# A decoder layer with sparse experts: a third buffer for raw expert weights, and a small load of its own for each slot's place and weight

## The chip, the cores and the metric

One core of a Trainium2 chip runs the whole kernel in one launch. The metric is the device time of one execution, in microseconds (us).

## The reference

The input is 32 sequences of 128 tokens with 256 channels (4096 tokens). Three blocks follow one another, each with a residual sum and a layer norm behind it: self-attention with 16 heads, cross-attention with one head onto a second input, and a feed-forward block that has an attention of its own and then a mixture of experts. The part that matters here is the last one:

```python
probs = jax.nn.softmax(h2 @ router_w, axis=-1)            # 8 experts
topw, topi = jax.lax.top_k(probs, 2)
topw = jax.nn.softmax(topw, axis=-1)
combine = jnp.sum(jax.nn.one_hot(topi, 8) * topw[..., None], axis=1)
shared = (silu(h2 @ sh_gate) * (h2 @ sh_up)) @ sh_down    # 256 -> 512 -> 256
gate = jnp.einsum('td,edf->etf', h2, e_gate)
up = jnp.einsum('td,edf->etf', h2, e_up)
eout = jnp.einsum('etf,efd->etd', jax.nn.silu(gate) * up, e_down)
out = layernorm(x2 + X + shared + jnp.einsum('etd,te->td', eout, combine))
```

Each token goes through the shared network and through the two experts that the router picks for it. All is float32.

## The kernel before, in words

**Two phases.** Phase A does the three attentions for 16 pairs of sequences by a schedule that is written out by hand. It is not touched. Phase B does the experts. It works in 55 *units* of 256 tokens, all with the same matrix products: first 13 units of the shared network (`BEFORE = 13`, a unit is a pair of sequences), then 39 *tiles* of routed tokens (`TILES`), then the last 3 shared units. A tile holds up to 256 tokens that go to one expert; which expert that is, is read at run time from `expert_table`, so its weights are loaded anew for each tile, 3 x 512 KB (gate, up, down).

**Products in split precision.** A float32 product is made of three products of rounded operands. ScalarE writes the rounded weights `we_hi` (`split`, L1257), VectorE the rest `we_lo` (`split_lo`, L1417), both from the raw weights `w_raw`, in the order down weights of tile n (kind 2), then gate and up weights of tile n+1 (kinds 0 and 1), all within unit n. TensorE then does, per unit n: gate and up for half the hidden channels (`gate_up(n, 0)`, 24 matmuls, L1204), the transposes of the tokens of unit n+1 (`turn(n+1)`, 4 matmuls, L1184), `gate_up(n, 1)`, and the down product of unit n-1 (`down_unit`, 24 matmuls, L1220). The activation between them passes ScalarE (silu and rounding, L1273 and L1280), VectorE (product, L1433) and GpSimd (the rest, `routed_lo`, L1561), and `down_unit(n)` waits for the last of it.

**Routing.** During the shared units VectorE works out each token's two slots. GpSimd scatters token rows into the scratch tensor `slots` by indirect DMAs (`scatter`, L1537). A row has 258 floats: 256 channels, its place in the output and its weight. `load_slots(i)` on SyncE loads the 256 rows of tile i into one of two buffers `slot_rows`. `read_meta(i)` on GpSimd then copies weight (L1556) and place (L1557, with a cast to an integer) into small rings of four, `slot_weight` and `slot_place`, so that the row buffer can be loaded again. When tile i has its down product, VectorE multiplies it by the weight into one of three `y_rows` (L1456), and GpSimd adds the rows to the scratch tensor `total` at their places by two indirect DMAs that accumulate (`add_tile`, L1572); it first waits until those of the tile before have landed (`y_added`).

**The raw weights.** `w_raw` has two buffers. `load_expert(i)` (L1137) fills buffer (i + 1) % 2. Tiles 0 and 1 are loaded early. After that SyncE goes through a loop, in order: wait for the transposes of tile i and for `meta_done` of tile i (L1153), `load_slots(i + 2)` (L1141), wait for the split of the down weights of tile i, the last reader of its buffer (L1135), `load_expert(i + 2)`. SyncE works in order, and all its loads go through one hardware queue (q1). The indirect DMAs of GpSimd go through another (q0).

**GpSimd's order** in unit n (tile i) is: `routed_lo(n, 0)`, `add_tile(i - 2)`, `read_meta(i + 1)`, `routed_lo(n, 1)`. At the end come the last two `add_tile`, then loads of `total` into `acc` that accumulate (L1593), and the last layer norm.

Of the kernel before, what the change touches and what calls it, by code (L numbers as in the profile page):

```python
# [17 lines left out]
F32 = mybir.dt.float32  # L18
# [29 lines left out]
ROW = D + 2  # L48
METAS = 4
KINDS = ("w_gate", "w_up", "w_down")  # L50
# [927 lines left out]
def phase_b(nc, t, scratch, sem, kept, all_stored, out):  # L978
# [6 lines left out]
    with ctx:  # L985
# [23 lines left out]
        y_rows = kept["late"][:, :].rearrange("p (i j d) -> p i j d", i=3, j=2)  # L1009
        place = sb("place", [P, B])  # L1010
        slot_weight = sb("slot_weight", [P, METAS, 2])
        slot_place = sb("slot_place", [P, METAS, 2], I32)

# [41 lines left out]
        h_loaded = [kept["loaded"], *(sem(f"h_loaded{g}") for g in range(1, GROUPS))]  # L1055
        raw_loaded = [sem(f"w_loaded{i}") for i in range(2)]
        rows_loaded = [sem(f"rows_loaded{i}") for i in range(2)]
# [16 lines left out]
        total_loaded = [sem(f"total_loaded{g}") for g in range(len(TOTALS))]  # L1074
        meta_done = sem("meta_done")
        var_done, eps_b_done, rstd_b_done, norm_done, out_stored = (
# [8 lines left out]
        def raw_of(use):  # L1085
            return kept["weights"] if use == 0 else w_raw[:, use % 2]

# [16 lines left out]

        totals = scratch["total"][0:P * B, :].rearrange("(p b) d -> p b d", p=P)

        def low_products(k):
# [6 lines left out]
        with nc.Block() as block:  # L1114

            @block.sync
            def _(sp):
                sp.dma_start(consts, t["route"]).then_inc(loaded, 16)
                sp.dma_start(tri[:, :], t["tri"]).then_inc(loaded, 16)
                sp.dma_start(place[:, :], t["place"]).then_inc(loaded, 16)  # L1120

                def load_rows(g):
                    b = slice(g * GB, (g + 1) * GB)
                    sp.dma_start(rows_of(b)[:, :, 0:D], scratch["h2"][:, b, :]).then_inc(h_loaded[g], 16)

                for g in range(1, GROUPS):
                    if g == GROUPS - 1:
                        all_stored(sp)
                    load_rows(g)

                def tile_rows(name, i):
                    return scratch[name][i * UT:(i + 1) * UT, :].rearrange("(j p) d -> p j d", p=P)

                def load_expert(i):
                    e = sp.value_load(expert_table[0:1, i:i + 1], min_val=1, max_val=E)  # L1135
                    for k, n in enumerate(KINDS):
                        sp.dma_start(w_raw[:, (i + 1) % 2, k, :], t[n][bass.ds(e, 1), :, :].rearrange("a p n -> (a p) n"))\  # L1137
                          .then_inc(raw_loaded[(i + 1) % 2], 16)

                def load_slots(i):  # L1140
                    sp.dma_start(slot_rows[:, i % 2, :, :], tile_rows("slots", i)).then_inc(rows_loaded[i % 2], 16)  # L1141

                sp.wait_ge(table_done, 1)
                load_expert(0)
                sp.wait_ge(w_lo_done, 3)
                load_expert(1)
                for i, batches in enumerate((B // 2, B // 2, B)):
                    sp.wait_ge(scattered[i], 16 * batches)
                for i in range(2):
                    load_slots(i)  # L1150
                for i in range(TILES - 2):
                    sp.wait_ge(turned_done, FIRST_TILE + i + 1)
                    sp.wait_ge(meta_done, 2 * i + 2)  # L1153
                    load_slots(i + 2)
                    sp.wait_ge(w_lo_done, split_count(FIRST_TILE + i, 2))
                    load_expert(i + 2)


                sp.wait_ge(y_added, 16 * 2 * TILES)
                sp.wait_ge(w_lo_done, split_count(AFTER_TILES - 1, 2))  # L1160

                b = slice(2 * BEFORE, B)
                sp.dma_start(acc[:, b, :], totals[:, b, :]).then_inc(total_loaded[total_of[BEFORE]], 16)
                for pair in range(PAIRS):
                    sp.wait_ge(norm_done, pair + 1)
                    sp.dma_start(out[:, 2 * pair:2 * pair + 2, :], acc[:, 2 * pair:2 * pair + 2, :]).then_inc(out_stored, 16)
                sp.wait_ge(out_stored, 16 * PAIRS)

            @block.tensor
            def _(pe):  # L1170
                def turn(n):
                    i = tile_of(n)
                    if i is None:
                        g = pair_of(n) * 2 // GB
                        pe.wait_ge(h_loaded[g], 16 if g else KEPT)
                        src = rows_of(slice(2 * pair_of(n), 2 * pair_of(n) + 2))
                    else:
                        pe.wait_ge(rows_loaded[i % 2], 16 * (i // 2 + 1))
                        src = slot_rows[:, i % 2, :, :]
# [66 lines left out]
            def _(act):  # L1246
                def split(n, kind):
                    i = tile_of(n)
                    w_hi, _ = weights_of(n)
                    use = 0 if i is None else i + 1  # L1250
                    act.wait_ge(*((kept["loaded"], KEPT) if use == 0 else (raw_loaded[use % 2], 48 * ((use + 1) // 2))))
# [5 lines left out]
                    act.activation(w_hi[:, kind, :], raw_of(use)[:, kind, :], ACT.Copy).then_inc(w_hi_done, 1)  # L1257

# [66 lines left out]
            def _(dve):  # L1325
# [86 lines left out]
                def split_lo(n, kind):  # L1412
# [3 lines left out]
                    dve.wait_ge(w_hi_done, split_count(n, kind))  # L1416
                    dve.tensor_tensor(w_lo[:, kind, :], raw_of(use)[:, kind, :], w_hi[:, kind, :].bitcast(F32),  # L1417
                                      ALU.subtract).then_inc(w_lo_done, 1)
# [21 lines left out]
                def read_down(n):  # L1440
# [10 lines left out]
                    else:  # L1451
                        if i >= 3:
                            dve.wait_ge(y_added, 16 * 2 * (i - 2))
                        dve.wait_ge(meta_done, 2 * i + 1)
                        for j in range(2):
                            ins = dve.tensor_scalar(y_rows[:, i % 3, j, :], src[:, j, :], slot_weight[:, i % METAS, j:j + 1], None, ALU.mult)  # L1456
                        ins.then_inc(down_read, 1)
# [60 lines left out]
            def _(pool):  # L1518
                pool.memset(ones[:, :], 1.0).then_inc(ones_b_set, 1)
                pool.memset(half_power[:, :], -0.5).then_inc(pool_set, 1)  # L1520
                pool.wait_ge(loaded, 16 * 3)
                pool.tensor_copy(kept["rows"][:, :, D], place[:, 0:GB]).then_inc(pool_set, 1)
                pool.tensor_copy(h_rows[:, :, D], place[:, GB:B]).then_inc(pool_set, 1)
                pool.wait_ge(pool_set, 3)
# [40 lines left out]
                def add_tile(i):  # L1565

                    pool.wait_ge(down_read, FIRST_TILE + i + 1)
                    pool.wait_ge(meta_done, 2 * i + 2)
                    if i > 0:
                        pool.wait_ge(y_added, 16 * 2 * i)  # L1570
                    for j in range(2):
                        pool.indirect_dma_start(  # L1572
                            out=scratch["total"], out_offset=bass.IndirectOffsetOnAxis(ap=slot_place[:, i % METAS, j:j + 1], axis=0),
                            in_=y_rows[:, i % 3, j, :], in_offset=None, compute_op=ALU.add).then_inc(y_added, 16)

                read_meta(0)
                for n in range(FIRST_TILE, AFTER_TILES):
                    i = tile_of(n)
                    routed_lo(n, 0)
                    if i >= 2:  # L1580
                        add_tile(i - 2)
                    if i + 1 < TILES:
                        read_meta(i + 1)
                    routed_lo(n, 1)
                add_tile(TILES - 2)
                add_tile(TILES - 1)

                pool.wait_ge(y_added, 16 * 2 * TILES)
                for g, pairs in enumerate(TOTALS):
# [51 lines left out]
def layout(inputs):  # L1641
# [29 lines left out]
    def route_constants():  # L1671
# [19 lines left out]
        "route": route_constants(),  # L1691
        "empty": (np.eye(1, ROW, D) * (B * S + np.arange(ROWS))[:, None]).astype(np.float32),
        "place": (B * np.arange(P)[:, None] + np.arange(B)).astype(np.float32),
        "wqk1": rows(np.concatenate([by_channel(a("L0_attn_Wq")), by_channel(a("L0_attn_Wk"))]).T),
# [30 lines left out]
```

## Time and profile before

| | us |
|---|---|
| median of 3 runs | 1162.86 (1160.27 to 1165.91) |
| the profiled execution's own time | 1166.36 |
| its span in the trace | 1164.6 |
| TensorE busy | 1080.5 (93% of the span) |
| VectorE, ScalarE, GpSimd busy | 800.5, 623.7, 572.5 |
| mean granted clock of TensorE | 0.971 of full speed |

How to read it: the busy time of TensorE is modelled and overlaps, so that 93% does not mean that nothing can be won. The span begins with phase A; phase B begins at about 615 us, and its 39 tiles take the time from about 740 to 1108 us. Of the DMAs of phase B the page gives the median time from issue to landing: 3.5, 4.5 and 6.6 us for the gate, up and down weights of one tile (512 KB each, all three issued within 1 us), 5.0 us for the slot rows (258 KB), 6.5 us for an accumulating indirect DMA.

### The profile page before, as it was taken

Reading aid. Unit: us, or ns where it says so; the run is one execution under the profiler, and the core shown is the slowest. Engines: PE = TensorE matmul, PEld = TensorE weight load, DVE = VectorE, ACT = ScalarE, POOL = GpSimd, SP = SyncE. Lnnn points to the kernel's source line nnn. Section 1 sums busy time; section 2 is a strip of 40 time slices with the busy share of each in tenths; the row PEclk is TensorE's granted clock in tenths of the full one; section 3 lists DMA queues with packets and bytes.
Section 4 is the critical chain, followed back from the end, with each engine's and each line's share of the span. In section 5 each row is a group of like instructions: output and inputs, shape, how many; then the busy total and the mean of one; then the engine's idle time right before and its main releaser. Section 6 shows DMA issues by size and latency. Waiting matters only on the chain. (4 is left out here: it accounts for less than half of the span.)

```text
span 1164.6 us, 32771 instructions
## 1 busy us (share of the span) xinstructions
PE 1080.5 (93%) x13012; PEld 1014.7 (87%) x13012; DVE 800.5 (69%) x1367; ACT 623.7 (54%) x1266; POOL 572.5 (49%) x620
## 2 busy tenths in 40 slices
PE   3889999999999999999777999999999999999992
PEld 3678888999888998999666999999999999999992
DVE  1668778777878777787646644567777777677646
ACT  1244555555555655566534333566666666666635
POOL 4243333344433334443210677356666676666664
PEclk8899999999999999999976999999999999999996
DMA  7585454444555444440304422267777777777648
GB/s 204 103 191 109 90 110 93 118 115 81 129 111 102 113 107 94 76 75 29 110 27 158 182 101 97 92 216 219 222 227 218 218 218 230 237 213 221 183 77 244
DMA packets 284071, 167.64 MB, mean 144 GB/s; under 512 B 210081, under 2 KB 255393, under 8 KB 283041
## 3 DMA queue, kind: packets, MB, share of 16 engines
q1 hardware_dynamic: 267456, 140.97, 44.1%
q0 software_dynamic: 14880, 22.09, 9.5%
q10 hardware_dynamic: 1584, 2.49, 0.6%
q8 instruction: 104, 1.70, 0.6%
q14 instruction: 47, 0.38, 0.1%
HBM read 121.66 MB, written 54.15 MB: 151 GB/s over the span
## 5 line engine op out<-in xcount | busy, mean ns | idle before, releaser
L1572 POOL DMA_INDIRECT total_scratch<-kept_late,slot_place x78 | 143.5, 1840 | 90.7 <-DMA total_scratch<-kept_late,slot_place 70.8
L1433 DVE TENSOR_TENSOR prod<-kept_weights,up 128x512 f32<-128x512 f32 x110 | 75.2, 684 | 145.0 <-ACT kept_weights L1273 145.0
L1561 POOL TENSOR_TENSOR act_lo<-prod,act_hi 128x512 fp32r<-128x512 f32 x78 | 120.5, 1596 | 40.5 <-ACT act_hi L1280 40.5
L1257 ACT ACTIVATE we_hi<-w_raw 128x1024 fp32r<-128x1024 f32 x117 | 117.9, 1048 | 26.6 <-DMA w_raw<-in_w_down 26.6
L1273 ACT ACTIVATE kept_weights<-gate 128x512 f32<-128x512 f32 x110 | 65.0, 591 | 110.7 <-PE up L1204 110.7
L1280 ACT ACTIVATE act_hi<-prod 128x512 fp32r<-128x512 f32 x110 | 69.5, 632 | 91.2 <-DVE prod L1433 89.9
L677 ACT ACTIVATE p3t<-psum 128x512 f32<-128x512 f32 x128 | 68.8, 595 | 88.6 <-PE psum L526 88.6
L928 POOL TENSOR_TENSOR ctx_lo<-ctx_t,ctx_hi 128x512 fp32r<-128x512 f32 x16 | 20.6, 1285 | 140.1 <-ACT ctx_hi L587 140.1
L1417 DVE TENSOR_TENSOR we_lo<-w_raw,we_hi 128x1024 fp32r<-128x1024 f32 x60 | 78.8, 1341 | 13.2 <-ACT we_hi L1257 11.6
L848 DVE TENSOR_REDUCE max<-psum 128x16 f32<-128x2048 f32 x32 | 73.3, 2292 | 18.2 <-PE psum L512 18.2
L367 PE MATMUL psum<-kept_room,x_hi 128*128 128x512 f32 (+1 forms) x256 | 63.4, 372 | 17.9 <-POOL x_lo L924 17.9
L1417 DVE TENSOR_TENSOR we_lo_place<-w_raw,we_hi 128x1024 fp32r<-128x1024 f32 x57 | 74.4, 1331 | 5.0 <-ACT we_hi L1257 3.5
L1204 PE MATMUL gate<-tok_hi,we_hi 128*128 128x256 f32 x312 | 67.5, 298 | 11.0 <-DVE we_lo L1417 7.9
L367 PEld LDWEIGHTS psum<-kept_room,x_hi 128*128 128x128 f32 x256 | 43.4, 202 | 25.7 <-issue 21.2
L1537 POOL DMA_INDIRECT slots_scratch<-h_rows,slot_index x56 | 55.0, 982 | 16.7 <-issue 12.5
L871 DVE RECIPROCAL rden<-psum 128x256 f32<-128x256 f32 x32 | 56.2, 1757 | 10.1 <-PE psum L539 10.1
L1204 PE MATMUL up<-tok_lo,we_hi 128*128 128x256 f32 x312 | 62.7, 283 | 0.0
L1204 PE MATMUL up<-tok_hi,we_hi 128*128 128x256 f32 x312 | 62.5, 282 | 0.0
L1204 PE MATMUL gate<-tok_lo,we_hi 128*128 128x256 f32 x312 | 62.5, 282 | 0.0
L1204 PEld LDWEIGHTS gate<-tok_hi,we_hi 128*128 128x128 f32 x312 | 47.6, 189 | 15.0 <-issue 14.7
L924 POOL TENSOR_TENSOR x_lo<-x_t,x_hi 128x512 fp32r<-128x512 f32 x16 | 20.4, 1275 | 67.0 <-ACT x_hi L583 66.9
L935 POOL TENSOR_TENSOR x_res<-x_res,b_o 128x512 f32<-128x512 f32 x16 | 21.0, 1311 | 61.0 <-DMA x_res<-in_x 61.0
(273 smaller groups left out, 3403.7 us busy)
## 6 DMA issues: line engine op xcount, KB each, us to landing
w_raw<-in_w_gate SPq DMA_DIRECT2D x39, 512.0 KB, 3.5
w_raw<-in_w_up SPq DMA_DIRECT2D x39, 512.0 KB, 4.5
w_raw<-in_w_down SPq DMA_DIRECT2D x39, 512.0 KB, 6.6
slots_scratch<-in_empty SPq DMA_DIRECT2D x39, 258.0 KB, 3.4
kept_weights<-slots_scratch SPq DMA_DIRECT2D x39, 258.0 KB, 5.0
x_t<-in_x_t SPq DMA_DIRECT2D x16, 256.0 KB, 3.3
q_scratch<-qk SPq DMA_DIRECT2D x16, 256.0 KB, 2.4
k_scratch<-qk SPq DMA_DIRECT2D x16, 256.0 KB, 2.9
```

What stands on the lines that cost most here:

```text
L367: mm = pe.matmul(dst, x(dk), y(dk), start=(n == 1), stop=(n == 3 * DK))
L677: act.activation(p3t[:, a, 4 * j:4 * j + 4, :], bank[f"s3t_{a}"][:, 512 * j:512 * (j + 1)].rearrange("p (h n) -> p h n", h=4), ACT.Exp)\
L848: half_step(dve.tensor_reduce(max3[:, a, :], bank[f"s3_{a}"].rearrange("p (h n) -> p h n", h=H), AX.X, ALU.max, negate=True))
L871: half_step(dve.reciprocal(rden3[:, a, :], bank[f"pv3_{a}"][:, DK * S:2 * DK * S]))
L1204: mm = pe.matmul(bank[:, fi * UT:(fi + 1) * UT], wp[:, kind, dk * DFF + f * P:dk * DFF + (f + 1) * P], hp[:, n % 2, dk, :], start=(m == 1) ...
L1257: act.activation(w_hi[:, kind, :], raw_of(use)[:, kind, :], ACT.Copy).then_inc(w_hi_done, 1)
L1273: act.activation(silu[:, h, :], gate[h][:, :], ACT.Silu).then_inc(silu_done, 1)
L1280: act.activation(act_hi[:, n % 2, h * FH:(h + 1) * FH, :], prod[:, h, :].rearrange("p (f n) -> p f n", f=FH), ACT.Copy).then_inc(act_hi_do ...
L1417: dve.tensor_tensor(w_lo[:, kind, :], raw_of(use)[:, kind, :], w_hi[:, kind, :].bitcast(F32), ALU.subtract).then_inc(w_lo_done, 1)
L1433: dve.tensor_tensor(prod[:, h, :], silu[:, h, :], up[h][:, :], ALU.mult).then_inc(prod_done, 1)
L1561: pool.tensor_tensor(act_lo[:, n % 2, h * FH:(h + 1) * FH, :], prod[:, h, :].rearrange("p (f n) -> p f n", f=FH), act_hi[:, n % 2, h * FH: ...
L1572: pool.indirect_dma_start(out=scratch["total"], out_offset=bass.IndirectOffsetOnAxis(ap=slot_place[:, i % METAS, j:j + 1], axis=0), in_=y_ ...
```

## The change

1. Raw weights get a third buffer. Its gate weights lie in a new tensor `raw_gate`, its up and down weights in the part of `h_rows` that held the rows of sequences 16 to 23, which were scattered and transposed by then. Uses of the buffers go round by three.
2. `load_slots(i)` also loads place and weight of the 256 slots into a ring `slot_meta` of six, by a DMA of its own: two runs of 8 bytes in each of 128 partitions. `rows_loaded` now counts 32 for a tile instead of 16. `read_meta` with its two copies goes, and `meta_done` with it. VectorE, and GpSimd's `add_tile`, read `slot_meta` in its place. Place is an integer from the start.
3. SyncE's loop has another order: `load_slots(i)` waits for the transposes of tile i-2 and, from tile 6, for the added rows of tile i-6; then the split of the down weights of tile i-2 is waited for, and `load_expert(i + 1)` follows. Tile 2 is loaded ahead of the loop.

```diff
-METAS = 4
+METAS = 6
+RAW_FROM = 12
...
-        place = sb("place", [P, B])
-        slot_weight = sb("slot_weight", [P, METAS, 2])
-        slot_place = sb("slot_place", [P, METAS, 2], I32)
+        place = sb("place", [P, B], I32)
+        slot_meta = sb("slot_meta", [P, METAS, 2, ROW - D])
+        raw_gate = sb("raw_gate", [P, WC])
+        sent = h_rows[:, :, :].rearrange("p b d -> p (b d)")[:, RAW_FROM * ROW:RAW_FROM * ROW + 2 * WC]
+        raws = [[w_raw[:, 1, k, :] for k in range(3)], [w_raw[:, 0, k, :] for k in range(3)],
+                [raw_gate[:, :], sent[:, 0:WC], sent[:, WC:2 * WC]]]
...
+        def added_upto(i):
+            return 2 * i
...
-                        sp.dma_start(w_raw[:, (i + 1) % 2, k, :], t[n][bass.ds(e, 1), :, :].rearrange("a p n -> (a p) n"))\
-                          .then_inc(raw_loaded[(i + 1) % 2], 16)
+                        sp.dma_start(raws[i % 3][k], t[n][bass.ds(e, 1), :, :].rearrange("a p n -> (a p) n"))\
+                          .then_inc(raw_loaded[i % 3], 16)
                 def load_slots(i):
+                    if i >= 2:
+                        sp.wait_ge(turned_done, FIRST_TILE + i - 1)
+                    if i >= METAS:
+                        sp.wait_ge(down_read, FIRST_TILE + i - METAS + 1)
+                        sp.wait_ge(y_added, 16 * added_upto(i - METAS + 1))
                     sp.dma_start(slot_rows[:, i % 2, :, :], tile_rows("slots", i)).then_inc(rows_loaded[i % 2], 16)
+                    sp.dma_start(slot_meta[:, i % METAS, :, :], tile_rows("slots", i)[:, :, D:ROW]).then_inc(rows_loaded[i % 2], 16)
                 sp.wait_ge(table_done, 1)
                 load_expert(0)
-                sp.wait_ge(w_lo_done, 3)
                 load_expert(1)
                 for i, batches in enumerate((B // 2, B // 2, B)):
                     sp.wait_ge(scattered[i], 16 * batches)
-                for i in range(2):
+                load_slots(0)
+                load_slots(1)
+                sp.wait_ge(turned_done, (GB + RAW_FROM + 2 * WC // ROW) // 2 + 1)
+                load_expert(2)
+                for i in range(2, TILES):
                     load_slots(i)
-                for i in range(TILES - 2):
-                    sp.wait_ge(turned_done, FIRST_TILE + i + 1)
-                    sp.wait_ge(meta_done, 2 * i + 2)
-                    load_slots(i + 2)
-                    sp.wait_ge(w_lo_done, split_count(FIRST_TILE + i, 2))
-                    load_expert(i + 2)
+                    if i + 1 < TILES:
+                        sp.wait_ge(w_lo_done, split_count(FIRST_TILE + i - 2, 2))
+                        load_expert(i + 1)
...
-                        pe.wait_ge(rows_loaded[i % 2], 16 * (i // 2 + 1))
+                        pe.wait_ge(rows_loaded[i % 2], 32 * (i // 2 + 1))
...
-                        dve.wait_ge(meta_done, 2 * i + 1)
+                        dve.wait_ge(rows_loaded[i % 2], 32 * (i // 2 + 1))
...
-                def read_meta(i):
-                    pool.wait_ge(rows_loaded[i % 2], 16 * (i // 2 + 1))
-                    if i >= METAS:
-                        k = i - METAS
-                        pool.wait_ge(down_read, FIRST_TILE + k + 1)
-                        pool.wait_ge(y_added, 16 * 2 * (k + 1))
-                    pool.tensor_copy(slot_weight[:, i % METAS, :], slot_rows[:, i % 2, :, D + 1]).then_inc(meta_done, 1)
-                    pool.tensor_copy(slot_place[:, i % METAS, :], slot_rows[:, i % 2, :, D]).then_inc(meta_done, 1)
...
                 def add_tile(i):
                     pool.wait_ge(down_read, FIRST_TILE + i + 1)
-                    pool.wait_ge(meta_done, 2 * i + 2)
+                    pool.wait_ge(rows_loaded[i % 2], 32 * (i // 2 + 1))
```

## Rows read from the trace of the kernel before

**Rows 1.** The page, part 1: engine, busy us, share of the span, instructions.

```profile
PE 1080.5 (93%) x13012; PEld 1014.7 (87%) x13012; DVE 800.5 (69%) x1367; ACT 623.7 (54%) x1266; POOL 572.5 (49%) x620
```

**Rows 2.** Busy us per stretch (PE, PEld, DVE, ACT, POOL), clock, DMA share, GB/s.

```profile
737.72:1105.85 368.13, 357.11 (x2964) 353.16 (x2965) 262.54 (x349) 232.47 (x349) 243.20 (x226) 1.00 0.72 211
```

**Rows 3.** Waits from 740 to 1110: engine and line, for whom, us, times, longest.

```profile
ACT we_hi L1257 <- DMA w_raw<-in_w_down: 26.6, 27, 2.4
...
PE gate L1204 <- DVE we_lo L1417: 7.9, 10, 1.6
```

**Rows 4.** The chain that ended last: start us, us, what, two tiles of it.

```profile
884.53 7.42 DMA w_raw<-in_w_down
891.97 1.07 ACT we_hi L1257
893.07 1.24 DVE we_lo L1417
894.44 1.67 PE gate L1204 x12
...
899.48 1.05 ACT we_hi L1257
900.55 1.50 DVE we_lo L1417
903.68 7.24 DMA w_raw<-in_w_down
```

**Rows 5.** PE in order of time: one tile's transposes, of 40 such rows these five.

```profile
737.72 0.66 PE L1184 MATMUL turned<-ident,kept_weights 128*128 128x128 f32 x4 [0.78 <-DMA kept_weights<-slots_scratch]
...
859.22 0.60 PE L1184 MATMUL turned<-ident,kept_weights 128*128 128x128 f32 x4
868.21 0.60 PE L1184 MATMUL turned<-ident,kept_weights 128*128 128x128 f32 x4
...
982.01 0.60 PE L1184 MATMUL turned<-ident,kept_weights 128*128 128x128 f32 x4
...
1105.85 0.60 PE L1184 MATMUL turned<-ident,h_rows 128*128 128x128 f32 x4
```

**Rows 6.** SyncE's queue in order of time: the first slot rows, two expert loads.

```profile
734.99 0.38 SPq L1141 DMA_DIRECT2D kept_weights<-slots_scratch  x1
...
978.36 0.34 SPq L1137 DMA_DIRECT2D w_raw<-in_w_gate  x1
...
987.39 0.34 SPq L1137 DMA_DIRECT2D w_raw<-in_w_gate  x1
```

**Rows 7.** GpSimd in order of time, one tile; last, idle before it and its releaser.

```profile
978.62 1.77 POOL L1572 DMA_INDIRECT total_scratch<-kept_late,slot_place  x1 [2.08 <-DMA total_scratch<-kept_late,slot_place]
980.69 1.55 POOL L1572 DMA_INDIRECT total_scratch<-kept_late,slot_place  x1 [0.30 <-issue]
981.94 1.87 POOL L1561 TENSOR_TENSOR act_lo<-prod,act_hi 128x512 fp32r<-128x512 f32 x1
...
987.90 1.75 POOL L1572 DMA_INDIRECT total_scratch<-kept_late,slot_place  x1 [2.33 <-DMA total_scratch<-kept_late,slot_place]
```

**Rows 8.** Small runs in phase A: eight loads of 512 runs of 64 bytes.

```profile
L329 SPq DMA_DIRECT2D vbd<-v_scratch x8: 485/486/2675, 299.3 to 305.9; - x8
...
DMA to landing us min/median/max: 2.5/2.5/4.9
```

**Rows 9.** The same loads: busy us per stretch as in Rows 2, DMA share second to last.

```profile
304.00:305.00 1.00, 1.00 (x10) 1.00 (x9) 0.87 (x2) 1.00 (x3) 1.00 (x2) 1.00 0.44 46
```

**Rows 10.** VectorE and GpSimd in order of time, where both read at once.

```profile
1041.62 2.08 DVE L1417 TENSOR_TENSOR we_lo_place<-w_raw,we_hi 128x1024 fp32r<-128x1024 f32 x1
...
1039.51 3.11 POOL L1561 TENSOR_TENSOR act_lo<-prod,act_hi 128x512 fp32r<-128x512 f32 x2
```

**Rows 11.** Groups from 740 to 1110: line, engine, operation, count, busy us, mean ns.

```profile
L1556 POOL COPY slot_weight<-kept_weights 128x2 f32<-128x2 f32 x38 | 30.3, 798 | 0.0
```

**Rows 12.** GpSimd at the end of the tiles: one accumulating DMA.

```profile
1109.57 2.36 POOL L1572 DMA_INDIRECT total_scratch<-kept_late,slot_place  x1 [0.15 <-issue]
```

More of the change, by code:

```diff
@@ L1055, in phase_b @@
         h_loaded = [kept["loaded"], *(sem(f"h_loaded{g}") for g in range(1, GROUPS))]
-        raw_loaded = [sem(f"w_loaded{i}") for i in range(2)]
+        raw_loaded = [sem(f"w_loaded{i}") for i in range(3)]
         rows_loaded = [sem(f"rows_loaded{i}") for i in range(2)]
@@ L1074, in phase_b @@
         total_loaded = [sem(f"total_loaded{g}") for g in range(len(TOTALS))]
-        meta_done = sem("meta_done")
         var_done, eps_b_done, rstd_b_done, norm_done, out_stored = (
@@ L1085, in raw_of @@
         def raw_of(use):
-            return kept["weights"] if use == 0 else w_raw[:, use % 2]
+            return [kept["weights"][:, k, :] for k in range(3)] if use == 0 else raws[(use - 1) % 3]
         FIRST_TILE, AFTER_TILES = BEFORE, BEFORE + TILES
@@ L1148, in _ @@
                     sp.wait_ge(scattered[i], 16 * batches)
-                for i in range(2):
-                    load_slots(i)
-                for i in range(TILES - 2):
-                    sp.wait_ge(turned_done, FIRST_TILE + i + 1)
-                    sp.wait_ge(meta_done, 2 * i + 2)
-                    load_slots(i + 2)
-                    sp.wait_ge(w_lo_done, split_count(FIRST_TILE + i, 2))
-                    load_expert(i + 2)
-                sp.wait_ge(y_added, 16 * 2 * TILES)
+                load_slots(0)
[3 more added lines that the diff above has]
+                for i in range(2, TILES):
+                    load_slots(i)
+                    if i + 1 < TILES:
+                        sp.wait_ge(w_lo_done, split_count(FIRST_TILE + i - 2, 2))
+                        load_expert(i + 1)
+                sp.wait_ge(y_added, 16 * added_upto(TILES))
                 sp.wait_ge(w_lo_done, split_count(AFTER_TILES - 1, 2))
@@ L1250, in split @@
                     use = 0 if i is None else i + 1
-                    act.wait_ge(*((kept["loaded"], KEPT) if use == 0 else (raw_loaded[use % 2], 48 * ((use + 1) // 2))))
+                    act.wait_ge(*((kept["loaded"], KEPT) if use == 0 else (raw_loaded[(use - 1) % 3], 48 * ((use - 1) // 3 + 1))))
                     if i is not None and i >= 2:
@@ L1256, in split @@
                             act.wait_ge(down_ready, n - 1)
-                    act.activation(w_hi[:, kind, :], raw_of(use)[:, kind, :], ACT.Copy).then_inc(w_hi_done, 1)
+                    act.activation(w_hi[:, kind, :], raw_of(use)[kind], ACT.Copy).then_inc(w_hi_done, 1)
                 def token_hi(n):
@@ L1416, in split_lo @@
                     dve.wait_ge(w_hi_done, split_count(n, kind))
-                    dve.tensor_tensor(w_lo[:, kind, :], raw_of(use)[:, kind, :], w_hi[:, kind, :].bitcast(F32),
+                    dve.tensor_tensor(w_lo[:, kind, :], raw_of(use)[kind], w_hi[:, kind, :].bitcast(F32),
                                       ALU.subtract).then_inc(w_lo_done, 1)
@@ L1452, in read_down @@
                         if i >= 3:
-                            dve.wait_ge(y_added, 16 * 2 * (i - 2))
-                        dve.wait_ge(meta_done, 2 * i + 1)
+                            dve.wait_ge(y_added, 16 * added_upto(i - 2))
+                        dve.wait_ge(rows_loaded[i % 2], 32 * (i // 2 + 1))
                         for j in range(2):
-                            ins = dve.tensor_scalar(y_rows[:, i % 3, j, :], src[:, j, :], slot_weight[:, i % METAS, j:j + 1], None, ALU.mult)
+                            ins = dve.tensor_scalar(y_rows[:, i % 3, j, :], src[:, j, :], slot_meta[:, i % METAS, j, 1:2], None, ALU.mult)
                         ins.then_inc(down_read, 1)
@@ L1521, in _ @@
                 pool.wait_ge(loaded, 16 * 3)
-                pool.tensor_copy(kept["rows"][:, :, D], place[:, 0:GB]).then_inc(pool_set, 1)
-                pool.tensor_copy(h_rows[:, :, D], place[:, GB:B]).then_inc(pool_set, 1)
+                pool.tensor_copy(kept["rows"][:, :, D].bitcast(I32), place[:, 0:GB]).then_inc(pool_set, 1)
+                pool.tensor_copy(h_rows[:, :, D].bitcast(I32), place[:, GB:B]).then_inc(pool_set, 1)
                 pool.wait_ge(pool_set, 3)
@@ L1567, in add_tile @@
                     pool.wait_ge(down_read, FIRST_TILE + i + 1)
-                    pool.wait_ge(meta_done, 2 * i + 2)
+                    pool.wait_ge(rows_loaded[i % 2], 32 * (i // 2 + 1))
                     if i > 0:
-                        pool.wait_ge(y_added, 16 * 2 * i)
+                        pool.wait_ge(y_added, 16 * added_upto(i))
                     for j in range(2):
                         pool.indirect_dma_start(
-                            out=scratch["total"], out_offset=bass.IndirectOffsetOnAxis(ap=slot_place[:, i % METAS, j:j + 1], axis=0),
+                            out=scratch["total"], out_offset=bass.IndirectOffsetOnAxis(ap=slot_meta[:, i % METAS, j, 0:1].bitcast(I32), axis=0),
                             in_=y_rows[:, i % 3, j, :], in_offset=None, compute_op=ALU.add).then_inc(y_added, 16)
-                read_meta(0)
                 for n in range(FIRST_TILE, AFTER_TILES):
@@ L1581, in _ @@
                         add_tile(i - 2)
-                    if i + 1 < TILES:
-                        read_meta(i + 1)
                     routed_lo(n, 1)
@@ L1586, in _ @@
                 add_tile(TILES - 1)
-                pool.wait_ge(y_added, 16 * 2 * TILES)
+                pool.wait_ge(y_added, 16 * added_upto(TILES))
                 for g, pairs in enumerate(TOTALS):
@@ L1691, in layout @@
         "route": route_constants(),
-        "empty": (np.eye(1, ROW, D) * (B * S + np.arange(ROWS))[:, None]).astype(np.float32),
-        "place": (B * np.arange(P)[:, None] + np.arange(B)).astype(np.float32),
+        "empty": (np.eye(1, ROW, D, dtype=np.int32) * (B * S + np.arange(ROWS, dtype=np.int32))[:, None]).view(np.float32),
+        "place": (B * np.arange(P)[:, None] + np.arange(B)).astype(np.int32),
         "wqk1": rows(np.concatenate([by_channel(a("L0_attn_Wq")), by_channel(a("L0_attn_Wk"))]).T),
```

## The prediction

> **What bounds the kernel now.** I read the page first: TensorE is busy 93% of the span, the others 69% and less [rows 1]. So time can only come from TensorE's waits, or from the ends of the phases. Only the tiles are touched, so I next took the stretch from the first tile's transposes to those of the first shared unit behind the tiles, 737.72 to 1105.85 us: 368.13 us for 39 tiles, 9.44 us each, with TensorE busy 357.11 us at a granted clock of 1.00 [rows 2, 5]. Then I read the starts of the transposes one by one, since one unit follows the other there. The quickest tiles take 8.99 us, as from 859.22 to 868.21 [rows 5], and then TensorE waits for nobody. A tile that takes longer waits for the rest of the gate weights from VectorE, and that work waits, over ScalarE, for the raw weights: 26.6 us of waiting on ScalarE in 27 of the tiles [rows 3].
>
> The chain of waits shows the loop that does it [rows 4]. Down weights are issued at 884.53 and take 7.42 us to land, ScalarE and VectorE split the gate weights (1.07 and 1.24 us), the gate products begin at 894.44, then come the two splits of the down weights, and at 903.68 down weights are issued again. That is 19.15 us for two tiles, 9.57 each, against 8.99 of matrix work. With two buffers a tile's load starts only when the tile two before it has been split, so this loop goes round once in two tiles and TensorE cannot be faster than it.
>
> **The change, part by part.** *The third buffer.* Tile i+1 is now issued after the split of tile i-2, where before it was after that of tile i-1: one unit, 9 us, earlier. The same loop now spreads over three tiles: 19.15 / 3 = 6.4 us per tile, below 8.99. So the stall goes whole, and the matrix work is late next. What does a tile then take? From below 8.99 us [rows 5]. From above 9.44, if something of the same size is right behind. I take 9.05, near the quick tiles, with 0.06 for an occasional short wait. Sum: 39 x (9.44 - 9.05) = 15.2 us; the ends are 17.5 us (all tiles at 8.99) and 0.
>
> *The DMA queues.* The DMA engines are busy 0.72 of the stretch [rows 2], 0.72 x 368.13 / 39 = 6.8 us per tile. The small load adds 256 runs of 8 bytes. The nearest rows are loads of 512 runs of 64 bytes, issued (305.9 - 299.3) / 7 = 0.94 us apart [rows 8] at a share of 0.44 [rows 9]: 0.41 us for 512 runs, so some 0.2 us for 256. 7.0 of 9.05 us leaves the engines idle for 2 us per tile: nothing on the path. Below, the cost is zero; above, the share in the row would be all due to latency and each run would cost as much whatever its size, still 0.4. SyncE pays one more issue of 0.49 us a tile [rows 8], and it waits most of the time.
>
> *What is queued behind the new waits on SyncE.* Tile i's slot rows now ask for the added rows of tile i-6, and the next expert load stands behind them. Adds of a tile start about 0.3 to 0.5 us behind an expert issue and the next tile's adds, which wait for their landing, start 9.3 us later (978.62 to 987.90) [rows 6, 7]. So the adds of tile i-6, issued in unit i-4, have landed when SyncE asks in unit i-3, or do so within a microsecond. The expert load behind is due only a unit later. Zero, with 8 us of cover. The slot rows themselves go out behind 1.5 MB of weights now, but are wanted some 18 us later.
>
> *GpSimd loses two copies a tile*, 0.8 us each [rows 11], partly beside each other. It waits 2.33 us for its adds right afterwards [rows 7]: the freed time becomes waiting. The wait for `meta_done` on SyncE stands before the slot rows, not between a split and its expert load. Both at zero. What they could give at most is that the last part of the activation is ready earlier, for which TensorE does not wait. The other readers (VectorE's factor, the offsets of the adds) wait for a count that the transposes have already waited for: zero.
>
> *The first tile.* Here alone slot rows are on the path: issued at 734.99, landed just before 737.72, TensorE idle 0.78 us for them [rows 5, 6]. The transposes now wait for the small load too, issued some 0.45 us later. The 64-byte loads land in 2.5 us at least and mostly, 4.9 at most [rows 8]: 737.9 or 740.3 against 737.7, so +0.3 to +2.7 us. I take +0.5, by the median and a little for the rows ahead of it. The Trainium skill ("DMA: Bandwidth & Descriptors", rules for kernel authors) speaks against such loads: below 64 KB one pays mostly overhead. By its fit of 2.0 us per DMA the small load would land at 737.4, before the rows, and this term would be zero; that fit is for DMAs issued from GpSimd, and no run here shows it for SyncE.
>
> *The end.* The adds of the third last tile start 0.15 us behind GpSimd's own product, at 1109.57 [rows 12], so no load held them. The chain of adds and the final norm move with TensorE. Zero.
>
> Net: -15.2 + 0.5 = -14.7 us. The profiled execution took 1166.36 us (1.8 us beside its span of 1164.6), so it would take 1151.7. It is 3.5 us above the median of the runs shown, 1162.86; the same 14.7 off that median gives 1148.2 us, my prediction.
>
> **Rivals.** *A: GpSimd and VectorE take the stall's place.* An add waits for the landing of the one before, and this one seems bound to the end of the weights' traffic: 987.90 is 9.54 us behind the expert issue at 978.36 and 0.51 behind the next at 987.39 [rows 6, 7]. If each tile takes 9.05, adds start 0.5 us behind an issue, the following product of GpSimd ends 5.2 us later (978.62 to 983.81), 5.7 behind the issue. The down product wants it at 985.3 or so: 982.01, plus the transposes (0.3) and half of the gate and up products (24 of 74 equal matmuls of 8.99, 2.9 us) [rows 5], that is 6.9 behind the issue. Cover is 1.2 us. Small loads that stretch the traffic by 0.2 us leave 1.0. But if the adds slip further, two products of GpSimd run back to back (3.11 us) and the split of the down weights beside them takes 2.08 us in place of 1.50 [rows 4, 10], which puts the gate weights late. The Trainium skill ("SBUF — State Buffer", who interferes with whom) has it that a VectorE instruction with two inputs in SBUF contends with a GpSimd one that reads SBUF; the trace agrees with its 2.08 against 1.50. For: the tiles around 980 take above 9.03. Against: their waits too are for weights. At 9.2 us a tile: 39 x 0.24 = 9.4, less 0.5: 1154.0.
>
> *B: no gain.* Expert loads are not earlier, because SyncE gets stuck at the adds of tile i-6, or they are and the traffic is merely spread. For it: all loads stand in one queue behind one waiting engine. Against: 8 us of cover, above. Time: 1162.9 + 0.5 = 1163.4.
>
> *C: slower, by the small runs.* An 8-byte run could cost far more than a 64-byte one. Then the queue never runs dry, and a tile takes 6.8 us plus the small load. From 2.6 us on (165 ns a run and engine; the row gives 0.41 x 16 / 512 = 13 ns) this is above 9.44. At 3.5 us: 10.3 a tile, 39 x 0.86 = +33.5, with the start 1196.9. For: no row shows runs of 8 bytes. Against: a factor of 13.
>
> **How the numbers follow.** Forecast 0.67 (its own range 1144 to 1152), A 0.17, B 0.09, C 0.07. About 0.5% (5.8 us) is what this measurement tells from no change. Faster: the forecast and nearly all of A, 0.83; same: B and the rest of A, 0.10; slower: C, 0.07. The range from 1144 to 1157 holds the forecast (17.5 us off and a little noise: 1144) and A with its noise; B and C are left out, 0.16.
>
> **What would show it.** Right: ScalarE no longer waits for the down weights at L1257 in the tiles; transposes 8.99 to 9.1 us apart all along; an expert issue every 9.0 us, landed more than 5 us before ScalarE wants it; DMA share near 0.77; GpSimd waits for its adds about 2 us in each tile; TensorE idle 1.0 to 1.5 us ahead of the first tile. A: splits of the down weights at 2.08 us in many tiles and a wait of TensorE for VectorE or GpSimd that no DMA stands behind. B: the waits for weights still there. C: issues on time, landings ever later. I am wrong altogether if the distance of the transposes stays at 9.4.

## The result: half of the forecast gain

| | us |
|---|---|
| median of the changed kernel, 5 runs | 1154.99 (1154.34 to 1157.68) |
| median of the kernel before, 5 runs | 1162.86 |
| ratio after / before | 0.9937 [0.9913, 0.9961] |
| profiled execution, before and after | 1166.36 and 1154.84 |
| span, before and after | 1164.6 and 1153.0 |

The change saves 7.9 us by the medians, between 4.5 and 10.1 by the interval, where 14.7 were forecast. The spans of the two profiled executions differ by 11.6 us, because the one of before took 3.5 us more than the median of its runs. They can be taken apart at the same marks as before. First TensorE, one tile's transposes, in order of time (start us, us, idle before it), for [rows 5]:

```profile
736.09 0.66 PE L1201 MATMUL turned<-ident,kept_weights 128*128 128x128 f32 x4 [1.02 <-DMA slot_meta<-slots_scratch]
...
900.00 0.60 PE L1201 MATMUL turned<-ident,kept_weights 128*128 128x128 f32 x4
909.26 0.60 PE L1201 MATMUL turned<-ident,kept_weights 128*128 128x128 f32 x4
918.47 0.60 PE L1201 MATMUL turned<-ident,kept_weights 128*128 128x128 f32 x4
...
1094.28 0.60 PE L1201 MATMUL turned<-ident,h_rows 128*128 128x128 f32 x4
```

The tiles take 1094.28 - 736.09 = 358.19 us, 9.18 each, where they took 368.13 and 9.44: 9.9 us of the 11.6. Another 1.6 us lie ahead of the first tile (737.72 against 736.09; this mark lies between 735.2 and 738.5 us in the traces of all kernels below, whatever their tiles do), and the end is the same (58.7 to 58.8 us behind the last mark in both). So the effect of the change is in the tiles. Some 2 us of the 9.9 can still be scatter of that one execution of before, since the medians differ by 7.9 only. The stretch and its waits (engine and line, for whom, us in total, times, longest), for [rows 2, 3]:

```profile
736.09:1094.28 358.19, 357.02 (x2964) 353.29 (x2965) 267.51 (x349) 229.20 (x349) 222.99 (x148) 1.00 0.76 218
```

```profile
POOL total_scratch L1580 <- DMA total_scratch<-kept_late,slot_meta: 53.9, 21, 3.3
...
POOL total_scratch L1580 <- DMA slot_meta<-slots_scratch: 32.9, 11, 3.7
POOL total_scratch L1580 <- issue: 18.3, 41, 3.9
PEld gate L1221 <- issue: 3.8, 16, 0.6
...
PE turned L1201 <- DMA slot_meta<-slots_scratch: 1.0, 1, 1.0
PE gate L1221 <- DVE we_lo L1434: 0.7, 2, 0.4
```

ScalarE's wait for raw weights, 26.6 us before, is gone altogether. TensorE's recorded idle time is down from 11.0 to 1.2 us. And yet a tile takes 9.18 us and not 9.0: in the middle of the stretch most take 9.19 to 9.27, many with a short gap of the weight loads ahead of the gate products (16 such waits on PEld). GpSimd waits for the landing of its adds as before. (The landing of the small load is named in 11 of these waits. In each of these too the next add starts 0.76 us behind the landing of the tile's second add, as in the waits that name the adds; so it is the adds that are waited for.)

What happens in such a tile is seen on three engines. GpSimd, VectorE and SyncE's queue in order of time:

```profile
906.88 1.85 POOL L1580 DMA_INDIRECT total_scratch<-kept_late,slot_meta  x1 [2.94 <-DMA total_scratch<-kept_late,slot_meta]
909.03 1.55 POOL L1580 DMA_INDIRECT total_scratch<-kept_late,slot_meta  x1 [0.30 <-issue]
910.04 3.12 POOL L1569 TENSOR_TENSOR act_lo<-prod,act_hi 128x512 fp32r<-128x512 f32 x2
```

```profile
912.43 1.83 DVE L1434 TENSOR_TENSOR we_lo<-w_raw,we_hi 128x1024 fp32r<-128x1024 f32 x1
914.18 2.35 DVE L1434 TENSOR_TENSOR we_lo_place<-w_raw,we_hi 128x1024 fp32r<-128x1024 f32 x2
```

```profile
905.77 0.36 SPq L1146 DMA_DIRECT2D raw_gate<-in_w_gate  x1
...
915.00 0.36 SPq L1146 DMA_DIRECT2D w_raw<-in_w_gate  x1
```

GpSimd's adds begin 1.1 us behind the expert issue and its second product of the unit comes behind them, so late that the next unit's first product follows with no gap (x2, 3.12 us, to 913.16). VectorE's split of the down weights runs beside it, takes 1.83 us where it takes 1.48 in a quick tile, and ends 1.1 us behind GpSimd. The gate split comes after it, and TensorE's first gate products of the next unit start late by a fraction of a microsecond:

```profile
915.54 0.47 PE L1221 MATMUL gate<-tok_hi,we_hi 128*128 128x256 f32 x2
```

This is 6.28 us behind the transposes at 909.26, where it is 6.15 to 6.17 us in every quick tile of this trace. Four such tiles, set beside a quick one matmul by matmul, differ nowhere else: the gate products start 0.13 to 0.16 us late, lose another 0.07 us or so, and all that follows is 0.2 us late. Over all tiles from the third on, the split of the down weights and the length of the tile go together: up to 1.67 us for the split, and the tile takes at most 9.06; 1.70 to 1.72, and it takes 9.10 or 9.11; 1.83 or more (22 tiles), and it takes 9.19 or more. In the whole stretch there are 28 such pairs of products, against 7 before.

### The profile page after: what moved, and what is told of

Same layout as the page of the kernel before. It is cut to its first block and busy times, and to the rows that moved or that the text cites. A ratio compares the mean times of both kernels' runs of the same rounds, so it can differ in the third digit from the quotient of the medians.

```text
span 1153.0 us, 32693 instructions
## 1 busy us (share of the span) xinstructions
PE 1076.8 (93%) x13012; PEld 1011.7 (88%) x13012; DVE 805.8 (70%) x1367; ACT 620.1 (54%) x1266; POOL 551.0 (48%) x542
## 5 line engine op out<-in xcount | busy, mean ns | idle before, releaser
L1580 POOL DMA_INDIRECT total_scratch<-kept_late,slot_meta x78 | 135.4, 1736 | 110.6 <-DMA total_scratch<-kept_late,slot_meta 58.5
L1274 ACT ACTIVATE we_hi<-w_raw 128x1024 fp32r<-128x1024 f32 x78 | 77.7, 1044 | 0.0
L872 DVE RECIPROCAL rden<-psum 128x256 f32<-128x256 f32 x32 | 56.2, 1757 | 10.1 <-PE psum L540 10.1
L1434 DVE TENSOR_TENSOR we_lo_place<-w_raw,we_hi 128x1024 fp32r<-128x1024 f32 x39 | 53.7, 1403 | 1.2 <-ACT we_hi L1274 0.3
L1434 DVE TENSOR_TENSOR we_lo<-w_raw,we_hi 128x1024 fp32r<-128x1024 f32 x39 | 53.4, 1396 | 1.2 <-ACT we_hi L1274 0.3
L1237 PE MATMUL down<-we_hi,act_hi 128*128 128x256 f32 x312 | 50.2, 283 | 0.0
```

The lines of the kernel that those rows point to most:

```text
L1237: mm = pe.matmul(down[n % 2][:, j * D:(j + 1) * D], ap[:, n % 2, f, j * P:(j + 1) * P], wp[:, 2, f * D:(f + 1) * D], start=(m == 1), stop= ...
L1274: act.activation(w_hi[:, kind, :], raw_of(use)[kind], ACT.Copy).then_inc(w_hi_done, 1)
L1434: dve.tensor_tensor(w_lo[:, kind, :], raw_of(use)[kind], w_hi[:, kind, :].bitcast(F32), ALU.subtract).then_inc(w_lo_done, 1)
L1580: pool.indirect_dma_start(out=scratch["total"], out_offset=bass.IndirectOffsetOnAxis(ap=slot_meta[:, i % METAS, j, 0:1].bitcast(I32), axis=0),
```

## Experiments

Medians are compared with runs of the kernel before on the same chip. "Per tile" is the distance of the same two marks in the trace, divided by 39. "Pairs of products" counts, between these marks, where two products of GpSimd follow one another with no gap.

| kernel | median us | ratio to before | per tile us | pairs of products |
|---|---|---|---|---|
| before | 1162.5 to 1162.9 | | 9.44 | 7 |
| changed | 1154.99 | 0.9937 [0.9913, 0.9961] | 9.18 | 28 |
| changed, again | 1156.26 | 0.9947 [0.9930, 0.9963] | 9.21 | 30 |
| third buffer alone | 1155.70 | 0.9941 [0.9918, 0.9964] | 9.18 | 18 |
| small load alone | 1160.95 | 0.9993 [0.9977, 1.0009] | 9.38 | 20 |
| gate weights first | 1172.67 | 1.0083 [1.0049, 1.0116] | 9.73 | 32 |
| half the adds | 1149.18 | 0.9892 [0.9869, 0.9915] | 9.02 | 0 |
| two totals | 1147.76 | 0.9871 [0.9853, 0.9889] | 9.02 | 0 |
| late issue | 1149.40 | 0.9885 [0.9869, 0.9902] | 9.08 | 0 |
| slots first | 1186.91 | 1.0216 [1.0190, 1.0241] | 9.94 | 34 |
| adds last | 1220.14 | 1.0495 [1.0476, 1.0515] | 10.69 | 0 |
| third buffer, late issue | 1149.56 | 0.9885 [0.9868, 0.9903] | 9.05 | 0 |
| late issue, slots between | 1148.95 | 0.9881 [0.9864, 0.9899] | 9.02 | 0 |

**The two parts of the change.** The first is `raws`, `raw_gate` and the new order of loads on the kernel before, with `read_meta` kept:

```diff
+                    sp.wait_ge(turned_done, FIRST_TILE + i - 1)
+                    sp.wait_ge(meta_done, 2 * i - 2)
                     load_slots(i)
+                    if i + 1 < TILES:
+                        sp.wait_ge(w_lo_done, split_count(FIRST_TILE + i - 2, 2))
+                        load_expert(i + 1)
```

> The third buffer alone, on the kernel before: slot rows as before, GpSimd's two small copies kept, no small load. Theory 1 (the small load's traffic lets the accumulating adds land later; GpSimd's two products then run back to back beside VectorE's split of the down weights, which takes 1.8 to 2.1 us and makes the gate weights 0.2 us late): adds land 0.3 to 0.6 us earlier, most tiles 9.0 to 9.1 us, 1150 to 1152 us. Theory 2 (any third buffer leaves VectorE at its own bound of 9.2 us a tile, whatever the adds do): 9.2 us a tile, 1154 to 1156 us.

Theory 1 falls as it stood: without the small load the tiles take the same 9.18 us. The adds are earlier, as it said: they start 5.9 us behind the unit's transposes in the mean, against 6.5 in the changed kernel. But GpSimd still makes its two copies, and from the start of the adds to the end of the product behind them it takes 5.5 us against 5.1, which gives back most of it. Here quick tiles (8.98 to 9.05 us, 20 of them) and slow ones (9.27 to 9.74, mostly 9.35) change places, where the changed kernel has a broad 9.2; the sum is the same.

The second is the changed kernel with `raws[i % 2]` and the order of loads of before:

> The small load and the ring of six alone, with two buffers for raw weights. Both theories: the loop over two buffers bounds the tiles again, 9.4 to 9.5 us, 1162 to 1166 us; if the small load were a cost on the path, above 1168. The first tile's transposes come 0.3 to 1 us later.

9.38 us a tile and a ratio whose interval holds 1: the small load and the lost copies together are worth nothing that can be measured. The whole gain is the third buffer's. No run has the one without the other, so what each is worth alone stays open; by the traces they pull against each other. With the small load and the earlier issue of slot rows that goes with it, adds start half a microsecond later in the unit (6.2 against 5.7 us in the mean, here against before), and without the copies GpSimd needs 0.3 us less behind them.

**Is it VectorE's order?** ScalarE and VectorE split gate and up weights of the next tile ahead of the down weights:

```diff
-                    if i is not None:
-                        split(n, 2)
                     if tile_next:
                         split(n + 1, 0)
                         split(n + 1, 1)
+                    if i is not None:
+                        split(n, 2)
```

> The changed kernel, with gate and up weights of the next tile split ahead of the down weights of this one, on ScalarE and VectorE. Theory 1: a slow split of the down weights no longer stands in front of the gate weights, 9.0 us a tile, 1147 to 1150 us. Rival: the expert load is issued 2.3 us later in the unit, the adds that are bound to its traffic slip by as much, and TensorE waits for GpSimd ahead of the down product instead: 1153 us or more, with waits of TensorE for L1569.

The rival came true, at 1172.67 us (the runs spread from 1161.77 to 1178.45). Whichever split stands first meets GpSimd's product (the gate split now takes 2.70 us at 870.73), and the adds slip with the later expert issue until TensorE waits ahead of the down product:

```profile
870.73 2.70 DVE L1443 TENSOR_TENSOR we_lo<-raw_gate,we_hi 128x1024 fp32r<-128x1024 f32 x1
```

```profile
PE down L1246 <- issue: 18.8, 29, 1.7
```

The row names no releaser ("issue"). The times do: each of these down products starts 0.10 us behind the end of the first product of a pair on GpSimd, the last thing that it needs (861.79 behind 861.69, to name one).

**Is it the adds?** One accumulating DMA per tile, `for j in range(1)`, and counts to match:

> The changed kernel with only the first of each tile's two accumulating DMAs: half of the routed rows are never added. Theory 1: GpSimd is free 1.9 us earlier in each tile, its products keep apart, the split of the down weights takes 1.5 us, tiles 9.0 us: 7 us less than the changed kernel, and some 4 us less at the end, where the adds are on the path: 1143 to 1146 us. Theory 2: tiles stay at 9.2 us, only the end is shorter: 1150 to 1152 us.

Tiles at 9.02 us and no pair of products: the adds it is. The end was not shorter, though, and I had expected 4 us: in the chain that ended last, TensorE's last units and the final norm stand where the adds stood. So the run took 1149.18 us and not the 1143 to 1146 of the expectation.

**Time, traffic or the wait?** Half the adds take away three things at once. Two scratch tensors for the sums take away only the wait:

```diff
-                    if i > 0:
-                        pool.wait_ge(y_added, 16 * added_upto(i))
+                    if i > 1:
+                        added(pool, i - 2)
...
-                            out=scratch["total"], out_offset=...
+                            out=scratch["total_odd" if i % 2 else "total"], out_offset=...
```

> The changed kernel with a second scratch tensor for the sums of odd tiles, so that a tile's adds wait for those of the tile two before it and no longer for the last one's; the odd sums are left out of the result. All adds and all DMA traffic stay. Theory 1, mended (the small load does not matter; the wait for the landing of the last tile's adds makes GpSimd late, its two products run back to back and slow VectorE's split of the down weights): adds start right behind GpSimd's first product, that split takes 1.5 us, tiles 9.02 us, 1148 to 1150 us. Theory 3 (what matters is GpSimd's own time for two adds, or the traffic of two adds, which half the adds took away as well): tiles 9.15 us or more, 1154 us or more.

9.02 us with all adds and all traffic, though an add takes 7.0 to 7.3 us to land in the median, no less than the 6.8 of the changed kernel: it is the wait of a tile's adds for the landing of the last tile's. This answers the question that decides.

**Can the adds land sooner?** Before the next expert load, SyncE waits for one more count:

```diff
                         sp.wait_ge(w_lo_done, split_count(FIRST_TILE + i - 2, 2))
+                        sp.wait_ge(act_hi_done, 2 * (FIRST_TILE + i - 2) + 2)
                         load_expert(i + 1)
```

> The changed kernel, with each expert load held back by some 2.8 us more, until ScalarE has rounded the second half of the same unit's activation. Theory 1, mended: adds that start before the weights' traffic land before it, so GpSimd waits less, tiles 9.0 to 9.1 us, 1149 to 1152 us. Rival (the landing of the adds is bound to the end of the weights' traffic wherever that lies): adds start 2.8 us later in the unit, TensorE waits for GpSimd ahead of the down product, 9.6 us or more a tile, 1170 us or more.

The rival is out. The weights go out 4.3 us behind the end of the down split, where they went out 0.7 us behind it; so the load is 3.6 us later and not 2.8. Adds that start ahead of the weights' traffic land in 4.7 us in the median and early enough, GpSimd waits 0.7 us for them in all the tiles instead of 87, and no pair of products is left. The later weights cost a little: slot rows, issued behind them, come late for TensorE four times.

```profile
PE turned L1202 <- DMA slot_meta<-slots_scratch: 2.8, 4, 1.1
```

**Two orders that went wrong.** Slot rows and small load ahead of the weights, right behind the split (`load_slots(i + 1)` between the wait and `load_expert(i + 1)`):

> The changed kernel, with slot rows and the small load issued ahead of the expert weights instead of behind them. If the adds land with the end of the weights: 0.5 us earlier in the unit is not to be had, since the weights then end later by as much: 9.15 to 9.2 us a tile, 1154 to 1156 us. If the small load behind the weights held them: 9.05 us, 1150 us.

Neither: 9.94 us a tile. The experiment moved more than it meant to. `load_slots` also waits for added rows, and that wait now stood between the split and the expert load, with nothing to cover it. SyncE's waits in this kernel:

```profile
SPq L1155 <- DMA total_scratch<-kept_late,slot_meta: 219.0, 33, 7.7
```

Expert issue and adds then follow one another in a ring: an add waits for the weights' traffic, the weights for the add. It says nothing on slot rows behind or ahead of weights, but it prices the cover that the change has there.

GpSimd's adds behind both products:

> The changed kernel with GpSimd's adds behind both products of the unit. Theory 1, mended: GpSimd no longer waits for a landing, but the adds now stand in front of the next unit's first product, which then runs beside VectorE's split of the down weights in every tile: that split takes 2 us, tiles 9.25 to 9.4 us, 1157 to 1163 us. If the landing wait as such is what costs: tiles 9.02, 1149 us.

The direction was right, the price was not: 10.69 us a tile. The next unit's first product stands behind two adds and begins when VectorE's split has already begun. The split still ends 1.1 us behind it and takes 3.49 us, where my expectation had built on 2:

```profile
906.61 3.49 DVE L1434 TENSOR_TENSOR we_lo_place<-w_raw,we_hi 128x1024 fp32r<-128x1024 f32 x1
```

```profile
907.14 1.87 POOL L1569 TENSOR_TENSOR act_lo<-prod,act_hi 128x512 fp32r<-128x512 f32 x1
```

**The small load again, and the best version.** The late issue on the third buffer alone, without the small load:

> The third buffer on the kernel before (copies by GpSimd, no small load), with the expert load held back until ScalarE has rounded the second half of the unit's activation. If the small load and the lost copies are worth nothing once the adds have their place in the unit: 9.02 to 9.08 us a tile, 1148 to 1150 us, as with the small load. If the copies cost GpSimd the place: products back to back again, 9.15 us or more, 1153 us or more.

1149.56 against 1149.40 us, 9.05 against 9.08 a tile: the small load, with the lost copies, is worth nothing here either.

The late issue with slot rows in the gap ahead of the weights:

```diff
                     sp.wait_ge(w_lo_done, split_count(FIRST_TILE + i - 2, 2))
+                    load_slots(i + 1)
+                    sp.wait_ge(act_hi_done, 2 * (FIRST_TILE + i - 2) + 2)
                     load_expert(i + 1)
```

> The changed kernel with the expert load held back as in the late issue, and slot rows and small load issued between the split of the down weights and that load, so that they no longer land behind the weights. The adds keep their place: 9.02 us a tile, no wait of TensorE for slot rows but the first, 1147 to 1149 us. If slot rows there get in the way of the adds' landing: GpSimd waits again, 1152 us or more.

> The changed kernel itself again, beside the two others: 1153 to 1157 us, 9.15 to 9.2 us a tile, GpSimd's two products back to back in more than half of the tiles.

1148.95 us against 1156.26 for the changed kernel on the same chip, 7.3 us or 0.6% less, and 0.9881 [0.9864, 0.9899] of the kernel before. TensorE has no recorded idle time left in the tiles. GpSimd's tile in this kernel, and VectorE's split:

```profile
901.30 2.35 POOL L1581 DMA_INDIRECT total_scratch<-kept_late,slot_meta  x1 [0.16 <-issue]
903.96 1.96 POOL L1581 DMA_INDIRECT total_scratch<-kept_late,slot_meta  x1 [0.31 <-issue]
905.84 1.40 POOL L1570 TENSOR_TENSOR act_lo<-prod,act_hi 128x512 fp32r<-128x512 f32 x1
908.87 1.30 POOL L1570 TENSOR_TENSOR act_lo<-prod,act_hi 128x512 fp32r<-128x512 f32 x1 [1.63 <-ACT act_hi L1298]
```

```profile
909.78 1.47 DVE L1435 TENSOR_TENSOR we_lo<-w_raw,we_hi 128x1024 fp32r<-128x1024 f32 x1
```

```profile
735.21:1086.84 351.63, 351.63 (x2964) 351.63 (x2965) 256.81 (x349) 229.22 (x349) 253.85 (x148) 1.00 0.83 222
```

The adds follow GpSimd's product at once, the second product waits for nobody, and GpSimd then idles 1.63 us until the next product is due. The expert load is issued at 906.49, 2.5 us behind the start of the second add; from issue to landing an add takes 5.2 us in the median, and 6.8 us in the changed kernel.

## Why the prediction was wrong

- **The bound now.** Right. The loop over two buffers held the tiles at 9.4 us; with a third buffer ScalarE's waits for weights are gone, and the third buffer with GpSimd's copies and no small load gives the whole gain.
- **"I take 9.05".** This is the step that failed. Measured 9.18: 9.9 us of span in the term where 15.2 stood. The net of the medians is 7.9 us against 14.7, and what the term lacks is the 0.2 us that most tiles lose ahead of the gate products. The other end of the term, 9.44, was bounded by "something of the same size right behind"; that something was there, and it was my rival A.
- **Rival A, 1154.0 us, chance 0.17.** It happened, at 1154.99 us. I gave it too little because I measured GpSimd's cover, 1.2 us, against the wrong deadline: the down product, 6.9 us behind an expert issue. The nearer one is GpSimd's own next product, whose input is ready at 911.44, 5.7 us behind the issue at 905.77. By my own sum the second product ended 5.7 us behind it. (The trace of before had it too: behind the issue at 978.36 that next product starts at 984.28, 5.9 us later.) The cover was 0 to 0.2 us, not 1.2, and the adds came at 1.1 us and not at 0.5. My slip of 0.2 us "leaves 1.0" counted on time that was not there. The quick tiles of before proved only that TensorE can run at 8.99; it seems that there GpSimd, once late, is given back its time by TensorE's next stall for weights; with the stalls gone, nothing pays it back. That last sentence is argued from the two traces; no run took it apart. Shown are its ends: with the landing wait gone (two totals) tiles take 9.02 us, and so they do with the weights issued later and slot rows ahead of them.
- **The DMA queues.** Right: 0.76 x 358.19 / 39 = 6.98 us of DMA time a tile, after 6.80, for 0.2 us forecast, and the runs with and without the small load come out alike in time. "Nothing on the path" holds for the sum alone: the adds start 0.6 us later in the unit than with the third buffer alone.
- **Waits on SyncE.** Right in the changed kernel, which shows no wait for added rows. The cover is real: where a run took it away, a tile cost 9.94 us. But "wanted some 18 us later" was wrong for slot rows. The small load is issued 1.9 us behind an expert issue (907.63 behind 905.77), lands 7.0 us later in the median, and TensorE wants it 12.7 us behind the issue, at the second of the next marks (918.47). An expert issue 3.6 us later was enough for TensorE to wait now and then.
- **The two copies.** Right for the copies and the small load together. The copies alone were not tried; "the freed time becomes waiting" overlooks that they stood between the adds and the product, where they cost GpSimd 0.3 to 0.4 us.
- **The first tile.** Right in size: idle 1.02 us against 0.78, for +0.5 forecast, so +0.2.
- **The end.** Right, unchanged to 0.1 us.

The Trainium skill ("SBUF — State Buffer", SBUF: two separate sides) has a sentence that would have priced the overlap of rival A: whichever of the two instructions starts first gets the shared pair of ports for the whole instruction, and the other fully blocks. The traces agree that VectorE blocks and does not merely slow down: a split alone takes 1.21 us in the median, and in each of the 13 traces the split that meets GpSimd's product ends 1.08 to 1.10 us behind the end of that product, however long it has run by then. They do not bear out that the first to start wins. With the adds last, the split starts ahead of the product (906.61 against 907.14) and still ends 1.09 us behind it; and with gate weights first, 32 splits have two products back to back beside them and end 1.09 us behind the second. By these records the measurement decides: the cost is how late GpSimd ends, and not a factor, nor the order of the starts. (The records of GpSimd overlap one another by some 0.4 us, so its starts are rough.)

## What to carry to other kernels

When a stall on the critical path goes, ask for each engine beside it what that stall gave back to it, and measure its cover against the next thing that the same engine has to start, not only against the consumer that the critical path names. With a third buffer the moment of a load is free to choose: the same 1.5 MB issued 3.6 us later in the period was worth about as much again as the buffer (6 to 7 us by the ratios), since a chain of small DMAs that wait for one another then lands ahead of the large ones (at the issue of 906.49 the second add lands 1.7 us behind it, the first of the weights 4.6). And a wait put in a queue costs by what stands behind it: the wait for added rows cost nothing ahead of slot rows, and a tile took 0.8 us more in the run where it stood ahead of weights.

## What the runs showed that I had not expected

- The price of the overlap between GpSimd's product and VectorE's split, of two inputs each, follows GpSimd's end: the split takes 1.21 us alone, 1.48 in quick tiles, 1.83 in the changed kernel, 3.49 with the adds last, and always ends 1.1 us behind the product.
- An accumulating indirect DMA that starts around the issue of the weights lands behind them. In the median of the tiles the second add lands 8.8 us behind the issue before the change and 9.4 after it, the down weights 7.4 and 7.0; and the next adds began 9.5 us behind the issue before the change [rows 6, 7], 10.2 behind it after the change (905.77 to 915.94). If it starts 5.2 us ahead of the issue (901.30 against 906.49), it is no longer waited for.
- Loads of 256 runs of 8 bytes beside 1.5 MB per tile cost nothing that could be measured, once GpSimd's copies were gone for them.
